# Sixteen conv cells and three convolutions in one kernel: images 0 and 1 normalised from a raw copy, the opening's work spread over three engines, own halves ahead of halo waits

## The reference

```python
# L0: a 4 by 4 lattice of cells. A cell concatenates up to 3 inputs of 16 channels, convolves 3x3 to 48,
# adds a bias, takes relu, and splits the result into (right, up, down), inputs of the neighbouring cells
outs[row] = split(relu(conv3x3(concat(ins), W[col, row]) + b[col, row]), 3)
# L1: a circular 3x3 convolution.  L2: cubic B-spline features (8) and silu of each pixel, 3x3 convolution.
# L3: a plain 3x3 convolution with bias.
# group norm: 8 groups of 2 channels; L0's takes its mean and variance over each image's 2 channels x 64 x 64
```

## Time and profile before

| | |
|---|---|
| median of 3 executions | 1261.64 us |
| the profiled execution, its own time | 1263.95 us |
| its span, first to last instruction | 1262.1 us |
| mean granted TensorE clock | 0.982 |
| TensorE matmuls | 1177.1 us busy (93%) |
| VectorE, ScalarE, GpSimd | 60%, 54%, 30% |
| HBM traffic over the span | 165 GB/s |

### The profile page before, as it was taken

How to read it: one execution, slowest core, us unless ns; L and a number is a source line. 1 busy time by engine, 2 the same in 40 slices (tenths; PEclk the granted TensorE clock), 3 DMA queues, 4 the chain that set the end, 5 groups by cost and what they waited for, 6 DMA issues and landing times.

```text
span 1262.1 us, 14781 instructions
## 1 busy us (share of the span) xinstructions
PE 1177.1 (93%) x5052; PEld 871.8 (69%) x5052; DVE 762.3 (60%) x967; ACT 676.3 (54%) x737; POOL 379.3 (30%) x553
## 2 busy tenths in 40 slices
PE   2988989989999999989999999998999987999995
PEld 1655667666666677766666677777777766777773
DVE  6898962456555522245655552236655789899952
ACT  2677854345445434445445444344444799789821
POOL 8231333424422012412122303634134442104212
PEclk9999999999999999999999999999999998999998
DMA  6899999999999968999999988978799414777873
GB/s 172 230 249 243 289 265 248 183 173 209 209 194 198 218 187 217 218 185 206 201 210 202 197 213 213 256 204 224 193 206 196 59 32 69 108 115 108 126 124 58
DMA packets 103342, 233.65 MB, mean 185 GB/s; under 512 B 35476, under 2 KB 48356, under 8 KB 94884
## 3 DMA queue, kind: packets, MB, share of 16 engines
q1 hardware_dynamic: 80768, 179.28, 65.6%
q0 software_dynamic: 16064, 24.70, 10.8%
q10 hardware_dynamic: 6436, 28.74, 7.3%
...
HBM read 123.59 MB, written 85.19 MB: 165 GB/s over the span
## 4 chain that ended last, share of the span: by engine, by line
PE 56%; SPq 17%; DVE 12%; DMA 5%; issue 5%; ACT 3%; POOL 2%; DVEq 0%; ACTq 0%; POOLq 0%
PE PB L1772 48%; SPq L830 14%; PE PB L1741 7%; DMA S<-lattice 2%; DVE F L1472 2%; DVE F L1484 2%; DMA F<-F 2%; DVE S L1609 1%; DVE S L1596 1%; DVE S L1602 1%; ACT F L1167 1%; DVE F L1589 1%; SPq L812 1%; SPq L861 1%; ACT F L1243 1%
## 5 line engine op out<-in xcount | busy, mean ns | idle before, releaser
L1772 PE MATMUL PB<-F,WA 128*96 128x512 f32 (+1 forms) x3792 | 917.8, 403 | 27.5 <-ACT S L1178 11.1
L1772 PEld LDWEIGHTS PB<-F,WA 128*96 128x96 f32 (+1 forms) x3792 | 662.7, 176 | 274.0 <-issue 18.8
L1178 ACT ACTIVATE S<-PB,BIAS 96x512 f32<-96x512 f32 (+1 forms) x320 | 211.6, 683 | 305.0 <-PE PB L1772 303.3
L1167 ACT ACTIVATE F<-S 128x2116 fp32r<-128x2116 f32 (+4 forms) x160 | 261.6, 1635 | 184.3 <-issue 67.5
L1472 DVE TENSOR_TENSOR F<-S,F 128x1089 fp32r<-128x1089 f32 (+2 forms) x80 | 121.4, 1518 | 171.0 <-ACT F L1167 170.0
L1474 DVE TENSOR_TENSOR F<-S,F 128x1058 fp32r<-128x1058 f32 x64 | 80.7, 1261 | 189.8 <-ACT F L1167 189.4
L1484 DVE CAST F<-F 64x528 fp32r<-64x528 f32 (+4 forms) x304 | 182.0, 648 | 3.5
L929 POOL DMA_DIRECT2D WA<-taps x76 | 57.0, 751 | 346.9 <-ACT S L1178 310.2
L1741 PE MATMUL PB<-F,WA 128*128 128x512 f32 x576 | 146.7, 412 | 13.9 <-DVE F L1589 13.9
L1741 PEld LDWEIGHTS PB<-F,WA 128*128 128x128 f32 x576 | 112.0, 196 | 42.9 <-issue 14.6
L1475 DVE TENSOR_TENSOR F<-S,F 64x1058 fp32r<-64x1058 f32 x64 | 79.8, 1247 | 0.0
...
...
## 6 DMA issues: line engine op xcount, KB each, us to landing
...
S<-lattice SPq DMA_DIRECT2D x158, 136.1 KB, 3.5
S<-lattice SPq DMA_DIRECT2D x72, 272.5 KB, 4.9
lattice<-S ACTq DMA_DIRECT2D x50, 272.5 KB, 4.8
...
lattice<-S SPq DMA_DIRECT2D x48, 272.5 KB, 4.1
S<-lattice SPq DMA_DIRECT2D x158, 70.1 KB, 3.5
```

The source lines that it names most:

```text
L1167: act.activation(piece_view(s, h, 0), raw_view(s, h), ACT.Copy).then_inc(hi_ready, 1)
L1178: act.activation(wide(to[:, at:at + TS])[:, :, 0:RX], pixels(RING_BANK[n % SLOTS_O][0:cell.rows, :]), ACT.Relu, bias=BIAS[0:cell.rows, k:k ...
L1772: last = nc.tensor.matmul(bank, WA[0:rows, first:first + cell.rows], wide(FZ[0:rows, i % SLOTS_F, base:base + TS])[:, :, 0:RX], start=j == ...
```

## The change

Images 0 and 1 no longer pass through `XN`: eight loads from `x` (four per image) bring their raw rows into partitions 64 to 127 of slots 0 and 1, and ScalarE and VectorE normalise them from there into partitions 0 to 63; VectorE multiplies the piece ends by a mask and clears two pad rows. `XN` is normalised in eight pieces by three engines (ScalarE 3, VectorE 3, GpSimd 2), and SP, no longer ScalarE's queue, stores it. Statistics are combined once more, so that scale and shift of images 0 and 1 exist on all partitions. SP takes half of cell 0's tap stores and half of its spreading transfers from GpSimd. The three constant loads become one. Whole-tile clears become clears of the pads; the clears of `W3` and the tail of `F` move to GpSimd. `turned_hi_part("cell1")` and `turned_lo_part("cell1")` move behind the splits of image 1. `single_step` is split, its six own matmuls before the halo wait, and the last `l3_step` has 12 `keep_warm` matmuls between the halves.

```diff
+        def copy_loads(b):
+
+            for r in range(2):
+                src = x[b].rearrange("c (i r) w -> r c i w", r=2)[r]
+                for s in range(2):
+                    first = b * PIECE + r * WD + s
+                    dst = flat[COPY_ROWS + r * HALO + s:COPY_ROWS + (r + 1) * HALO:2, first:first + HT // 2 * WD]
+                    yield dst.rearrange("c (i w) -> c i w", w=WD), src
+
+        def copy_part(b, lower):
+
+            first = b * PIECE + (WD if lower else 0)
+            rows = flat[COPY_ROWS:P, first:first + (RQ * 2 * WD if lower else COPY_SIZE)]
+            return rows.rearrange("p (q f) -> p q f", f=2 * WD)[:, :, 0:WD + 1:2]
+
+        def image_part(b, lower):
+
+            raw = raw_slot(b)[0:COPY_ROWS]
+            return wide(raw[:, EVEN:PATCH] if lower else raw[:, 0:EVEN])
...
-        def direct_loads(b):
-
-            rows = slice(b * C, (b + 1) * C)
-            even, odd = (XN[rows, r * PIECE:(r + 1) * PIECE].rearrange("c (s f) -> c s f", s=2) for r in range(2))
-            raw = raw_slot(b)
-            even_rows, odd_rows = raw[0:HALO], raw[HALO:2 * HALO]
-            yield even_rows[:, 0:PATCH], even[:, :, 0:PATCH]
-            yield odd_rows[:, 0:EVEN], odd[:, :, TS:PATCH]
-            yield odd_rows[:, EVEN:PATCH], odd[:, :, 0:TS]
...
             sp.wait_ge(turned, TURN_AT["cell0"])
+            sp.wait_ge(turned_hi, TURN_AT["cell0"])
+            sp.wait_ge(turned_lo, TURN_AT["cell0"])
+            for dst, src in first_half(tap_stores("cell0")):
+                sp.dma_start(dst, src).then_inc(tp0_stored, 16)
+            sp.wait_ge(kr_clear, 1)
+            for dst, src in copy_loads(0):
+                sp.dma_start(dst, src).then_inc(copy_loaded[0], 16)
             load_taps(2)
+            sp.wait_ge(tp0_stored, dma_total(first_half(tap_stores("cell0"))))
+            sp.wait_ge(tp_stored, tp_after["cell0"])
+            for dst, src in first_half(cell_spread(cells[0])):
+                sp.dma_start(dst, src).then_inc(w0_loaded, 16)
             sp.wait_ge(xn_act, 1)
             sp.wait_ge(xn_dve, 1)
+            sp.wait_ge(xn_pool, 1)
+            for i in range(2):
+                for dst, src in input_stores(i):
+                    sp.dma_start(dst, src).then_inc(input_stored[i], 16)
...
             for s in range(STEPS):
                 k, b = divmod(s, B)
                 q, before = halves_before[s] % SLOTS_K, last_user[s]
-                if s == 0:
-                    sp.wait_ge(kr_clear, 1)
+                if s in INPUT_PARTS[0:2]:
+                    sp.wait_ge(input_stored[INPUT_PARTS.index(s)], 2 * 16)
                 if before is not None and COPIES[cells[before // B].kind]:
                     sp.wait_ge(raw_read, copied_before[before + 1])
                 elif before is not None:
                     sp.wait_ge(lo_ready, pieces_before[before + 1])
-                if s == INPUT_PARTS[0]:
-                    for i in range(2):
-                        sp.wait_ge(input_stored[i], 2 * 16)
-                        sp.wait_ge(image_loaded[i], loads_after[i])
                 if k:
                     sp.wait_ge(image_stored[b], 16 * stores_before[k])
-                for dst, src in direct_loads(s) if s < INPUT_PARTS[0] else input_loads(s):
+                for dst, src in input_loads(s) if s >= 2 else ():
                     sp.dma_start(dst, src).then_inc(image_loaded[q], 16)
...
-            pool.memset(flat[:, 0:2 * PIECE], 0.0).then_inc(kr_clear, 1)
-            pool.memset(ST[:, :, :], 0.0).then_inc(st_clear, 1)
+            pieces = XN.rearrange("p (r f) -> p r f", r=2)
+            for start in (-1, SEG):
+                pool.memset(pieces[:, :, start + RW:start + LEAD:RW], 0.0)
+                pool.memset(pieces[:, :, start + LEAD:start + TOP], 0.0)
+                pool.memset(pieces[:, :, start + HOFF + RW:start + SEG:RW], 0.0)
+            pool.memset(pieces[:, :, SEG - 1:SEG + 1], 0.0).then_inc(xn_clear, 1)
+            pool.memset(W3[:, :, :, :].bitcast(F32), 0.0).then_inc(wa_clear, 1)
+            for start in (0, SEG + 1):
+                pool.memset(ST[:, :, start:start + 1], 0.0)
+                pool.memset(ST[:, :, start + RW:start + LEAD:RW], 0.0)
+                pool.memset(ST[:, :, start + LEAD:start + TOP], 0.0)
+                pool.memset(ST[:, :, start + HOFF + RW:start + SEG:RW], 0.0)
+            pool.memset(ST[:, :, SEG:SEG + 1], 0.0).then_inc(st_clear, 1)
+            pool.memset(FZ[:, :, 2 * PIECE:FSLOT].bitcast(F32), 0.0).then_inc(wa_clear, 1)
             pool.wait_ge(pool_const, 1)
...
-            store_taps("cell0")
-            norm(slice(1, 2), slice(0, 1), 1)
+            pool.wait_ge(turned_hi, TURN_AT["cell0"])
+            pool.wait_ge(turned_lo, TURN_AT["cell0"])
+            for dst, src in second_half(tap_stores("cell0")):
+                pool.dma_start(dst, src).then_inc(tp_stored, 16)
+            norm(slice(0, 3), slice(0, 3), 1)
+            pool.wait_ge(norm_ready, 1)
+            for r, s, h in XN_ORDER[6:8]:
+                last = pool.tensor_scalar(xn_rows(r, s, h), channel_rows(r, s, h), RS[:, 2:3], NBI[:, 2:3],
+                                          ALU.mult, ALU.add)
+            last.then_inc(xn_pool, 1)
+            pool.wait_ge(tp0_stored, dma_total(first_half(tap_stores("cell0"))))
+            pool.wait_ge(tp_stored, tp_after["cell0"])
+            for dst, src in second_half(cell_spread(cells[0])):
+                pool.dma_start(dst, src).then_inc(w0_spread, 16)
             clear_taps("cell1")
-            for dst, src in cell_spread(cells[0]):
-                pool.dma_start(dst, src).then_inc(w0_loaded, 16)
             store_taps("cell1")
...
-            act.dma_start(IDF[:, :], consts[0:NG * C, P:P + NG * C]).then_inc(idf_loaded, 16)
-            act.dma_start(CB[:, :], consts[:, P + NG * C:P + NG * C + CB_COLUMNS]).then_inc(const_loaded, 16)
-            act.dma_start(G[:, :], consts[:, 0:P]).then_inc(const_loaded, 16)
+            act.dma_start(CONST, consts[:, 0:P + NG * C + CB_COLUMNS]).then_inc(const_loaded, 16)
...
+            for s in range(2):
+                eye = consts[s:s + 1, P:P + 2].broadcast_to([HALO, 2])
+                act.dma_start(MASK[s:COPY_ROWS:2, :], eye).then_inc(mask_loaded, 16)
+            act.wait_ge(pool_const, 1)
+            act.activation(VE[:, 0:1], TWOS[:, :], ACT.Copy)
...
+            def upper_rows(b):
+
+                rows = slice(COPY_ROWS, P)
+                act.wait_ge(copy_loaded[b], dma_total(copy_loads(b)))
+                last = normalise(image_part(b, False), copy_part(b, False), b, rows)
+                if b:
+                    last = normalise(image_part(b, True), copy_part(b, True), b, rows)
+                last.then_inc(upper_ready, 1)
+
             def split_hi(s, h):
 
                 i = pieces_before[s] + h
-                if h == 0:
+                if s < 2:
+                    act.wait_ge(image_ready, s + 1)
+                elif h == 0:
                     act.wait_ge(image_loaded[halves_before[s] % SLOTS_K], loads_after[s])
...
             turned_hi_part("cell0")
+            act.wait_ge(kr_clear, 1)
+            for dst, src in copy_loads(1):
+                act.dma_start(dst, src).then_inc(copy_loaded[1], 16)
             act.wait_ge(norm_ready, 1)
             act.wait_ge(xn_clear, 1)
-            for r, s, h in XN_ORDER[0::2]:
-                last = normalise(xn_rows(r, s, h), channel_rows(r, s, h), 0)
+            for r, s, h in XN_ORDER[0:3]:
+                last = normalise(xn_rows(r, s, h), channel_rows(r, s, h), 2)
             last.then_inc(xn_act, 1)
-            act.wait_ge(xn_act, 1)
-            act.wait_ge(xn_dve, 1)
-            for i in range(2):
-                for dst, src in input_stores(i):
-                    act.dma_start(dst, src).then_inc(input_stored[i], 16)
+            upper_rows(0)
+            split_hi(0, 0)
+            upper_rows(1)
+            split_hi(1, 0)
             turned_hi_part("cell1")
-            for i in range(2):
-                split_hi(piece_step(i), i - pieces_before[piece_step(i)])
             act.wait_ge(st_clear, 1)
...
+            slots = flat[:, 0:2 * PIECE].rearrange("p (q f) -> p q f", q=2)
+            nc.vector.memset(slots[COPY_ROWS:P, :, 0:WD + 1], 0.0)
+            nc.vector.memset(slots[COPY_ROWS:P, :, HT // 2 * WD:PIECE], 0.0)
+            nc.vector.memset(slots[0:COPY_ROWS, :, SEG + LEAD:SEG + HOFF], 0.0).then_inc(kr_clear, 1)
             nc.vector.memset(WT[:, :, :].bitcast(F32), 0.0).then_inc(wt_clear, 1)
-            nc.vector.memset(XN, 0.0).then_inc(xn_clear, 1)
-
-            def clear_weights():
-
-                for first in (960, 2016, 2496, 2976):
-                    nc.vector.memset(WA[4 * C:P, first:first + 96].bitcast(F32), 0.0)
-                nc.vector.memset(FZ[:, :, 2 * PIECE:FSLOT].bitcast(F32), 0.0)
-                nc.vector.memset(W1[4 * C:P, :, 2:4].bitcast(F32), 0.0)
```

(73 more changed lines are left out.)

53 lines of the change are left out of this document (39 added, 14 removed).

## The result

The changed kernel takes 1251.70 us (median of 5 runs, 1249.25 to 1253.45) where the kernel before, run beside it, takes 1262.22 (5 runs, 1259.15 to 1265.6): the ratio is 0.9924, 95% interval 0.9904 to 0.9944. Two later sets of runs gave 0.9908 (0.9877 to 0.9938) and 0.9919 (0.9893 to 0.9944). The profiled execution took 1253.06 us with a span of 1251.3, which is 10.9 and 10.8 less than before. The forecast was 10.6.

A forecast was written before the change was run, and what follows sets the result against it. To 110 us, SP's lattice-load issues and VectorE were taken to bound the kernel, with DMA 96% busy behind the opening. Head 5.6 + circular stage 1.4 + end 3.6 = 10.6, so 1261.64 becomes 1251.0 us, range 1245 to 1258.

The forecast's parts named there:

- XN: Opening, normalising by three engines: GpSimd's two pieces at 2.2 us each, complete at 20.3 us, one us later than before.
- Image 2: Opening: stores issued at 20.4 us, first pair landed at 25.3, TensorE has it near 35.2 against 40.88; head 5.6.
- the rival of GpSimd being quick: Opening: GpSimd's pieces at 1.1 us each, nothing shared; head 7.8 us, total time 1248.3 us; chance 0.12.
- the rival of the load stream: Behind the opening: first store pair needs 9 us, image 2 gains about 1; total time 1255.6 us; chance 0.15.
- The stall of ScalarE at cell 2's taps: Opening, waiting for the clear of WT: 0 to 2 us, covered by two images TensorE has in stock.
- Image 0 and the weights: Opening: copies land at 20 us, image ready near 25.3; cell 0's weights release the first matmul at 27.0 against 33.44.
- The short-runs rival: Opening: copy loads with 256-byte runs go one after another at 8.2 us, image 0 at 46; 1274.6 us; chance 0.05.
- Shared operands: Opening: GpSimd's two pieces and VectorE's three take turns, ending about 22.3 us; head 3.6, total 1253.0 us; chance 0.15.
- That the lead is carried whole: After the opening: steps are periodic, so what starts them earlier moves them whole; head 5.6 us.
- The circular stage, 1.4: Own halves first: six of twelve matmuls run inside the 2.90 us halo wait, gaining 1.4 us; bounds 0 and 1.9.
- The end, 3.6: Last step: six matmuls, twelve keep_warm, six at 0.26 us; 1.6 replaces 5.15, gaining 3.6, or 2.6 at 0.43 each.
- the rival that the end gives nothing: Last step: clock already fallen at 1243.3 us, 24 matmuls at 0.43 take 10.3; total time 1254.6 us; chance 0.05.

The follow-up runs named there:

- both pairs waited for: Changed kernel with step 2's lattice loads waiting for both pairs of XN stores, not the first alone: 1248.62 us, and 1249.44 us when run again.
- two of the variants with the same order of taps: Changed kernel with 12 keep_warm matmuls ahead of image 2's (1248.98 us), and with XN's eight pieces on ScalarE and VectorE, none on GpSimd (1251.82 us).
- the opening alone: Changed kernel with own halves back behind the halo waits in both stages and without the 12 keep_warm matmuls at the end: 1251.76 us, ratio 0.9935.

## Why the prediction was right, point by point

**Scale and shift.** Within the 0.7 of the forecast: ready at 16.14 (15.94 + 0.20) against 15.9, though the clear of 3.69 us is gone. VectorE now waits for x (0.67 us at 8.97) instead, its statistics end only 0.4 us earlier, and the larger operation on GpSimd (0.88 us, 0.58 before) and the second matmul spend that.

**XN.** Mis-sized. GpSimd's pieces take 1.16 us, the cheap end of 1.1 to 2.2; I had chosen the row of strided small operations; the cost per element, 2.3 ns, is that of the other row, 1296 elements at 2.2. The Trainium skill (GPSIMD Engine Reference, "3.1 Elementwise — side-by-side cycle accounting") has about 2.6 cycles an element, at the 1.2 GHz that the page gives: an estimate of 1.11 us for 512. The trace is close to it, but the page has that figure for an operation with two inputs and 1.8 cycles (0.77 us for 512) as the best case; the piece has one input and the trace doesn't reach the best case. VectorE's pieces were mis-read too: the 0.84 us was a mean that held one piece of 1.73, beside GpSimd's memset at 16.32; the others took 0.55 to 0.69. XN came 1.7 us earlier than forecast.

**Image 2.** The mechanism was right and one term wrong. I gave three load issues 1.4 us and 4 us of landing; they took 3.5 and 4.2, since the 545 KB pair was in flight. The comparison with both pairs waited for shows that this is contention: there nine issues take 4.02 us instead of 7.30. SP also wasn't done with its half of the spread when XN was complete, as I had it, but 0.4 us after. The loads start 1.7 us earlier than forecast (23.58 against 25.3) and lose 2.3 us from there. That image 2 came at 35.40 for a forecast of 35.2 is partly luck: these two errors nearly cancel, and my own terms add up to 34.5 (25.3 + 1.4 + 4 + 3.8), which I had rounded up on the way. So the rival of GpSimd being quick was right in its duration and wrong in what it gives (7.8), and the rival of the load stream was right in its place and too high in its price. The stall of ScalarE at cell 2's taps stayed under TensorE's stock in the changed kernel's three traces (0.05 to 1.57 us), but not in two of the variants with the same order of taps (3.90 and 4.17): this sign of being wrong is close to coming true in single executions.

**Image 0 and the weights.** The copies landed in 3.4 to 3.5 us (median of four, both queues), not in 4.1 to 8.2, and the weights released the first matmul, as forecast, 2.4 us earlier; in the second of the three executions VectorE's casts did, at 24.70. The short-runs rival fell: instead of 8.2 us each, one after another, four copies landed within 3.6 us each and overlapped. Loads of 136.1 KB from the lattice landed in 2.9 us (median of six, some of them beside the 545 KB pair), so some 0.6 us may be the price of the 256-byte runs.

**Shared operands.** The rival fell for these pieces: 1.87 us for three beside GpSimd's two, where three alone take about 1.5; one of them is 0.4 longer, none waits for a whole piece of GpSimd's. The Trainium skill (SBUF — State Buffer, "SBUF: two separate sides") limits its rule to VectorE operations in a two-port mode or with two inputs from SBUF. The pieces have one input and take 1.1 ns an element (0.55/512), no faster than the two-input operation of the earlier trace rows (2.36/2112 = 1.1), so I take them to be in no faster mode. By that rule they block nobody, and the trace agrees but for the 0.4 us; the case for the rival was weaker than the 0.15 I gave it.

**That the lead is carried whole.** Not shown, and too strong for a single execution: 5.5 at image 2, 3.0 to 5.6 at 1011.82 in the changed kernel's three traces and 6.1 to 9.2 in the three others with its opening. What makes it so between 60 and 400 us was not isolated.

**The circular stage, 1.4.** Near in the profiled execution (1.20), not borne out as a price. The wait of 1.41 us belonged to twelve matmuls that took 4.39 in that execution. Unsplit kernels gained 1.19 and 0.39 over the stretch, split ones 0.22 to 3.15 with a median of 0.60, and the unsplit kernel was no slower. TensorE gains 2.9 us at first with the split, the upper end of what the prediction gave it, but 1.0 to 2.1 of that is gone again by 1058.34 in its three traces; that ScalarE and VectorE pace the stage is argued from this. The bound of 0 that the prediction names is nearer; up to about 1 us can't be excluded.

**The end, 3.6.** Right in mechanism, and in size where the clock held (the prediction's "nothing computes" there is true of TensorE; VectorE was busy for 1.82 us). From the start of the halo issues, at which the own half can start, to the end of the last matmuls it was 10.28 us before (1243.33 to 1253.61, and 10.2 in the opening alone), and is 6.46 in the profiled execution (1237.00 to 1243.46), 3.8 less. But in seven of the twelve traces with the own half first, those six took 2.0 to 2.8 us instead of 1.71. There the extra twelve run slow as well and hold the last six back by about 1.0 us (they start at 1242.90; without the extra ones they start 4.80 behind the own half, which here would be 1241.87): 7.42 us (1237.07 to 1244.49), 2.9 less. Without them it is 7.73 (1236.40 to 1244.13), 2.6 less, which is the lower value that the prediction gave for this case. So the split carries most of the term, and `keep_warm` 0.3 us (one trace against one) where the clock has already fallen; where it hasn't, no run without them shows their worth. This is also what became of the rival that the end gives nothing: its condition, a clock fallen by then, held in seven of twelve traces, but its price was wrong, since from the start of the own half to the last matmul it took 7.4 us and not 10.3.

By the measured terms the sum is 5.1 + 1.2 + 4.5 = 10.8 for the profiled execution, of which the 0.7 behind the last matmul was in no term of the forecast. That 10.8 came so near to 10.6 is in part luck, with leads that differ by several us between executions. On the mean of executions I would now write 5 to 8 for the opening, 0 to 1 for the circular stage and about 3 for the end.
